# First transfers, warm-up products and one fill, rearranged at the head of a three-block transformer kernel

## The reference

```
Qh = split(layernorm(x) @ Wq.T + bq)      # 16 heads of 8
Kh = split(ctx @ Wk.T + bk);  Vh = split(ctx @ Wv.T + bv)
scores = einsum('bhqd,bhkd->bhqk', Qh, Kh) / sqrt(8)
attn = softmax(scores - max(scores));  attn = clip(attn, 1e-12)
attn = attn / sum(attn)
x = x + merge(einsum('bhqk,bhkd->bhqd', attn, Vh)) @ Wo.T + bo
```

## Time and profile before

| | |
|---|---|
| median of 3 runs | 210.49 us (210.32 to 210.79) |
| the profiled execution's own time | 210.37 us |
| its span, first to last instruction | 208.4 us |
| PE / DVE / ACT / POOL busy | 92% / 70% / 69% / 39% of the span |
| chain that ended last, by engine | PE 73%, DVE 13%, ACT 4%, DMA 3% |

### The profile page before, as it was taken

One profiled execution on the slowest core, in us unless ns is written; L12 is line 12 of the kernel. 1 busy time (PEld: TensorE's weight loads), 2 busy tenths in 40 slices (PEclk: granted clock), 3 DMA queues, 4 the chain that ended last, 5 costly groups with the idle time before them and its releaser, 6 DMA issues.

```text
span 208.4 us, 6357 instructions
## 1 busy us (share of the span) xinstructions
PE 190.9 (92%) x2558; PEld 132.3 (63%) x2559; DVE 145.7 (70%) x263; ACT 143.6 (69%) x321; POOL 81.5 (39%) x113
## 2 busy tenths in 40 slices
PE   4889899799999989999999999999879999999991
PEld 1335437255555545554554666897858998999981
DVE  5296488999999988999999944756984438222220
ACT  4768684488989897786796977686674545446660
POOL 6223679989899991110201001420000005078400
PEclk9999999999999999999999999999999999999999
DMA  5835332336437422327887750500000000000000
GB/s 119 285 151 216 118 98 89 93 94 228 159 101 198 122 81 82 97 67 234 277 296 211 213 190 6 203 2 0 3 0 3 0 0 13 3 0 5 0 0 20
DMA packets 8688, 21.24 MB, mean 102 GB/s; under 512 B 1664, under 2 KB 2784, under 8 KB 8656
## 3 DMA queue, kind: packets, MB, share of 16 engines
q1 hardware_dynamic: 7344, 19.47, 29.1%
q0 software_dynamic: 592, 0.74, 1.6%
q10 hardware_dynamic: 720, 0.59, 0.9%
HBM read 17.52 MB, written 3.28 MB: 100 GB/s over the span
## 4 chain that ended last, share of the span: by engine, by line
PE 73%; DVE 13%; ACT 4%; DMA 3%; issue 2%; POOL 2%; ACTq 1%; DVEq 0%
PE ps L1267 15%; PE ps L1516 13%; PE ps L1549 10%; PE ps L1248 10%; PE ps L1208 6%; PE ps L1113 4%; DVE mx L600 4%; DMA wks<-in_wk 3%; PE ps L1120 2%; PE ps L1407 2%; PE ps L1132 2%; POOL wr L496 1%; DVE sm L711 1%; PE ps L1413 1%; DVE kst L709 1%
## 5 line engine op out<-in xcount | busy, mean ns | idle before, releaser
L1025 ACT ACTIVATE ex<-ps 128x512 f32<-128x512 f32 x128 | 69.5, 595 | 15.7 <-PE ps L1248 12.8
L600 DVE TENSOR_REDUCE mx<-ps 128x2 f32<-128x1024 f32 x64 | 74.9, 1218 | 7.7 <-PE ps L1208 7.7
L1267 PE MATMUL ps<-ex,vau 128*9 128x128 f32 x1024 | 40.0, 274 | 0.5 <-ACT oS L1037 0.4
L1516 PE MATMUL ps<-xT,w1s 128*128 128x128 f32 x256 | 34.4, 278 | 0.2
L1516 PEld LDWEIGHTS ps<-xT,w1s 128*128 128x128 f32 x256 | 31.1, 192 | 1.6 <-ACT cT L1048 0.8
L1267 PEld LDWEIGHTS ps<-ex,vau 128*9 128x9 f32 x1024 | 22.1, 90 | 15.7 <-ACT ex L1025 11.8
L806 DVE SCALAR_TENSOR_TENSOR xs<-ps,wr,xs 128x128 f32<-128x128 f32 x32 | 11.2, 350 | 28.6 <-PE ps L1549 28.3
L1048 ACT ACTIVATE cT<-ps,b1s 128x128 f32<-128x128 f32 x64 | 18.2, 370 | 13.8 <-PE ps L1516 13.8
L1048 ACT ACTIVATE ex<-ps,b1s 128x128 f32<-128x128 f32 x64 | 18.1, 369 | 13.0 <-PE ps L1516 12.9
L1208 PE MATMUL ps<-kst,qst 64*128 64x512 bf16 x128 | 25.0, 381 | 1.9 <-DVE mx L600 1.8
L1248 PE MATMUL ps<-qst,kst 64*128 64x128 bf16 x512 | 25.5, 217 | 0.5 <-ACT ex L1025 0.4
(11 more groups left out here) (211 smaller groups left out, 255.3 us busy)
## 6 DMA issues: line engine op xcount, KB each, us to landing
kst<-parts_d SPq DMA_DIRECT2D x84, 64.0 KB
w1s<-in_w SPq DMA_DIRECT2D x8, 512.0 KB, 4.1
kst<-in_w SPq DMA_DIRECT2D x8, 512.0 KB, 4.8
parts_d<-w1s SPq DMA_DIRECT2D x4, 768.0 KB, 3.8
cT<-in_ctxT SPq DMA_DIRECT2D x3, 512.0 KB, 5.7
cT<-in_ctxT SPq DMA_DIRECT2D x2, 256.0 KB, 4.8
picks<-in_pick ACTq DMA_DIRECT2D x1, 384.0 KB, 5.3
qkvs<-in_qkvw POOLq DMA_DIRECT2D x1, 192.0 KB, 3.6
```

Of the source, the lines that this page charges most:

```text
L600: dve.tensor_reduce(out=mx2[:, b, 2 * pair:2 * pair + 2, f], in_=ps[:, bank:bank + 2, :], axis=AX.X, op=ALU.max).then_inc(s["redA"], 1)
L1025: act.activation(ex[:, e % NE, :], ps[:, EBANK["exp", e], :], ACT.Exp, scale=SCALE).then_inc(s["exp"], 1)
L1267: last = pe.matmul(ps[32 * j:32 * j + DK + 1, 7, 128 * hg:128 * hg + 128], vau[:, NK * b + c, GH * hg + j, :], ex[:, (2 * t + j % 2) % NE, ...
L1516: last = pe.matmul(ps[:, SELF[j % 2], 128 * n:128 * n + 128], w1s[:, f0:f0 + 128], xT[:, (b % B) * S:(b % B + 1) * S], start=True, stop=True)
```

## The change

- SP issues context piece 0 ahead of `x`; ACT issues `wks` ahead of `cols` and `ident`.
- VectorE's fill of pairs 2 and 3 (2048 words) becomes three memsets: 256 words of pair 3, its other 768, the 1024 of pair 2. The first raises the semaphore that TensorE waits for, the last the one that SP waits for.
- TensorE runs eight warm-up products instead of five, on those 256 words, and `keys(0)` ahead of `turn_first`.
- ScalarE's two fills of 2048 words go; GpSimd fills pairs 4 to 7 with one memset of 4096 words, between L446 and its wait for the queries' parts.

```diff
-        N_WARM = 5
+        N_WARM = 8
@@ sync
+            sp.dma_start(cT[:, 0, 0:512], ctxT[0, :, 0:512]).then_inc(d_c[0], 16)
             sp.dma_start(xs[:], x.rearrange("b s d -> s b d")).then_inc(d_x, 16)
-            sp.dma_start(cT[:, 0, 0:512], ctxT[0, :, 0:512]).then_inc(d_c[0], 16)
             sp.dma_start(cT[:, 0, 512:1024], ctxT[0, :, 512:1024]).then_inc(d_c[1], 16)
...
-                    sp.wait_ge(s["onesD"], 1)
+                    sp.wait_ge(s["onesD"], 2)
@@ gpsimd
-            pool.memset(expo[:, 4:5].bitcast(i32), MINUS_ONES2)
...
             pool.tensor_scalar(blbk[:], blocks[:], cols[:, 1:2], None, ALU.mult)
+            pool.memset(kst[:, 0, 4:8, :].bitcast(i32), MINUS_ONES2).then_inc(s["onesA"], 1)
             pool.wait_ge(s["qparts"], 1)
@@ vector
-            dve.memset(kst[:, 0, ON_CHIP:4, :].bitcast(i32), MINUS_ONES2).then_inc(s["onesD"], 1)
+            dve.memset(kst[:, 0, 3, 0:512].bitcast(i32), MINUS_ONES2).then_inc(s["onesD"], 1)
+            dve.memset(kst[:, 0, 3, 512:CTX].bitcast(i32), MINUS_ONES2)
+            dve.memset(kst[:, 0, 2, :].bitcast(i32), MINUS_ONES2).then_inc(s["onesD"], 1)
             dve.wait_ge(d_x, 16)
             layer_norm(0)
@@ scalar
+            act.dma_start(wks[:], wk).then_inc(d_wk, 16)
             act.dma_start(cols[:], bias).then_inc(d_cols, 16)
             act.dma_start(ident[:], ident_in).then_inc(d_id, 16)
-            act.dma_start(wks[:], wk).then_inc(d_wk, 16)
...
-            act.wait_ge(s["pool"], 2)
-            for p in (4, 6):
-                last = act.activation(kst[:, 0, p:p + 2, :].bitcast(fp32).rearrange("p r k -> p (r k)"),
-                                      expo[:, 4:5].broadcast_to([128, CTX]), ACT.Copy)
-            last.then_inc(s["onesA"], 1)
@@ tensor
-                pe.matmul(ps[:, 3, :], kst[:, 0, ON_CHIP, 0:128], kst[:, 0, ON_CHIP, 0:512], start=True, stop=True)
-            turn_first()
+                pe.matmul(ps[:, 3, :], kst[:, 0, 3, 0:128], kst[:, 0, 3, 0:512], start=True, stop=True)
             pe.wait_ge(d_wk, 16)
             keys(0)
+            turn_first()
             keys(1)
```

## The result

The changed kernel takes 214.88 us (median of 4 runs, 214.48 to 223.71) against 210.64 for the kernel before: 1.0193 times as long, 95% interval 1.0169 to 1.0217. The profiled execution took 215.06 us, its span 213.1 against 208.4. The three others have a median of 214.70: the change costs 4.1 us, twice the 2.0 that were forecast.

A forecast was written before the change was run, and what follows sets the result against it. The prediction took the head's chain through the layer norm and first `k_parts` to `key_rows(0)` as the bound. 210.37 us plus 2.0 lost to the held cast gave 212.4, 212.5 as a median, range 210.0 to 214.6.

The forecast's parts named there:

- What bounds the head: First 14 us: `key_rows(0)` waits for the first `k_parts`, behind a layer norm whose 3.0 us of slack the change uses up.
- Transfers: Head of the queues: `x`, now behind context piece 0, lands at about 5.7 us; piece 0 and `wks` around 5.
- X: Time at which VectorE can start the layer norm's statistics: 3.09 us before, forecast 5.7.
- The norm: VectorE's layer norm: its own chain stays 3.79 us, so `k_parts(0)` may start at 9.52 us, against 9.91.
- Fill: GpSimd's memset of 4096 words: 3.45 us long, from 9.25 to 12.7 us.
- The hold: VectorE's cast L566 waits for the rest of GpSimd's memset, 2.4 us, making the first `k_parts` 2.0 us late.
- the maximum of the earlier trace: A VectorE maximum out of PSUM, read as 1.23 us wholly inside a GpSimd fill: that form isn't held.
- The clock: TensorE's pace in the head: the main case, chance 0.42, had a fast clock, with 211.8 to 213.6 us.
- The sum: Whole kernel: 210.37 us profiled plus 2.0 gives 212.4, or 212.5 as a median.
- the rival: TensorE slow when `key_rows(0)` starts, costing 1.8 us on top of the cast's wait: 213.6 to 215.4, chance 0.25.

The follow-up runs named there:

- a1_filler: Changed kernel with 14 more unused products on TensorE between `queries` and `key_rows(0)`: 211.95 us, ratio 1.0062 to the kernel before.
- a2: Changed kernel with GpSimd's fill moved: 3072 words ahead of its power for the first layer norm, 1024 behind `qsq`: 210.24 us, ratio 0.9973.
- a3: Changed kernel with the two fills of 2048 words back on ScalarE and GpSimd's memset out: 210.15 us, ratio 0.9962.
- b3: a2 with five unused products between `keys(0)` and `turn_first` and four between `queries` and `key_rows(0)`: 211.26 us, ratio 1.0040.
- c1: Kernel before, `x` still first, with `wks` at the head of ScalarE's queue and ten early warm-up products: 213.44 us, ratio 1.0050.
- b1: Changed kernel with GpSimd's fill of 4096 words cut into 16 memsets of 256 words in the same place: 215.36 us, ratio 1.0221.
- b4: Kernel before with only the early warm-up: VectorE's fill in three memsets, nine products from 1.18 us on: 211.07 us, ratio 1.0030.
- c3: a2 without any warm-up product (`N_WARM = 0`): 212.65 us.
- d1: Kernel before with one line moved, `cols` behind `wks` in ScalarE's queue: 209.80 us, ratio 0.9953.
- a4_before_fill: Kernel before with only the fill moved from ScalarE to GpSimd, in the place the change gives it: 210.71 us, ratio 1.0022.
- b2: Changed kernel with half of GpSimd's fill (2048 words) in its place and the other half behind `qsq`: 212.56 us, ratio 1.0110.
- c2: Kernel before with one edit, `wks` at the head of ScalarE's queue: 210.88 us, ratio 1.0033.

## Why the prediction was wrong, by its steps

*What bounds the head.* Right: the layer norm, which had 3 us of slack, became the bound, and `k_parts(0)` behind it. *Transfers.* X was given as 5.7 (5.0 to 6.8) and is 5.44; `keys(0)` at 5.04 (5.1). *The norm.* `k_parts(0)` starts at X + 3.46 and not X + 3.82: the transposes ran at the fast level (0.44 us in place of 0.69), and the subtraction began 0.08 us ahead of the end of the copy. *Fill.* 3.45 forecast, 3.51 measured; start at X + 3.31 for X + 3.55. *The hold.* 2.4 forecast, 2.43 measured, and it ends with the fill as the rows of L540 had said. The rule of the Trainium skill ("SBUF — State Buffer", "Who interferes with whom"), that a VectorE cast in a two-port mode and a GpSimd instruction shut each other out for a whole instruction, agrees with the long memset here: 2.86 in place of 0.43. One reading on the way was off: the maximum of the earlier trace rows lay not wholly inside the fill, which ended at 24.35, 0.34 us ahead of it. Beside 0.9 us of the fill it took its usual 1.23, so the conclusion stands. Together these steps give `key_rows(0)` 1.41 us late, forecast 2.0; a1_filler, in which only they are left, came out at 211.95, and the forecast was 212.5.

*The clock* is the step that failed, twice. The sum has no term for it: the clock was to stay up through the pause ahead of `key_rows(0)`. It stood only as a rival, "if it is slow when `key_rows(0)` starts", given 0.25 against 0.42 for a clock that stays. The three executions of the ratio took 214.5 to 215.1, as the rival would have them (213.6 to 215.4), and the trace shows the clock falling 0.4 us behind a pause that the forecast had itself worked out ("up to 3.4 us"; 3.60 measured). The pause looked like a place where nothing is lost, since the chain waits for VectorE there. And the rival's price was put at 1.8 us, half of a slow stretch as long as the one before had. The stretch was 6.8 us long, not 3.6, and it cost 3.2: 1.4 us of the error come from that. The forecast borrowed the length from a place where TensorE had been at work, with two short pauses, for 4 us already; that this is why it was shorter there is not shown. With the terms as measured the sum is 212.5 - 0.6 (`x` and the norm came sooner than forecast) + 3.2 (the clock) = 215.1, and the traced execution took 215.06. The median of 214.88 lies 0.3 above the range given, which ended at 214.6, inside the rival's own.

That the gain in the better runs is small (a2, a3) is the layer norm again: of 1.98 us by which `keys(0)` came sooner, 1.0 reached VectorE.

*Still open:* why the clock rises by 7 us in some traces and between 10 and 20 in others of nearly the same order, and what happened in b3's and c1's high runs. The kernel before has high runs too: none of 19 beside b1 to b4, but two of nine at 215.0 and 215.4 beside c1 to c3, and four of 17 at 211.8 to 212.5 beside d1. The page "TensorE: Matmul & The Clock Gate", Part 1, of the Trainium skill says that the rise falls at different points from run to run. The spread of b4 and a4_before_fill would fit that, 209.84 to 212.44 and 210.36 to 213.78 for one program each, but no program was traced twice, so no run here shows the rise itself move.

## What to carry to other kernels

A transfer moved to the front pushes another back: work out how long the displaced one's own chain is (here 3.8 us of layer norm) and what stands behind it on each engine. An engine that waits "for free" is not free if it is TensorE in front of a dense stretch: such a pause turned a loss of 1.4 us into 4.1. And before work goes to GpSimd because it idles, look at which doubled-rate VectorE operations it will run beside; splitting it into pieces that follow each other without a wait doesn't help (b1), while doing half of it later does shorten the hold (b2).

## What was not expected of the hardware

- Sixteen memsets of 256 words, issued back to back, held VectorE's cast for 3.0 us, until the last had ended; the cast never got in between.
- The fall of the clock is not tied to the pause in one way. In the changed kernel it came when TensorE had gone back to work: `key_rows(0)` began at 13.41, and the stretch from 13 to 14 us has a mean granted clock of 0.91, the next ones 0.50.

```profile
13.00:14.00 1.00, 0.59 (x6) 0.25 (x6) 0.95 (x3) 0.00 (x0) 0.00 (x0) 0.91 0.04 16
15.00:16.00 1.00, 1.00 (x2) 0.00 (x0) 0.93 (x3) 0.66 (x1) 0.92 (x2) 0.50 0.00 0
```

  In b1, whose TensorE is idle from 9.97 to 14.17, it fell within the pause, at about 12.5:

```profile
12.00:13.00 1.00, 0.00 (x0) 0.00 (x0) 1.00 (x1) 0.00 (x0) 1.00 (x5) 0.76 0.61 246
13.00:14.00 1.00, 0.00 (x0) 0.00 (x0) 0.97 (x3) 0.00 (x0) 0.02 (x1) 0.50 0.18 74
```

- Nor does the length of the last pause decide it. In the traces of a3 and b2 the clock fell 0.2 and 1.1 us behind pauses of 1.92 and 1.90 us; in d1's it stayed up through one of 2.13 us.
- 64 KB at the third place of a queue landed 1.5 us later than at the second: `wks` took 5.3 us to land from its issue in the kernel before and 4.3 in d1, where it was issued 0.5 us sooner, so it gained 1.5 in all for 2 KB moved behind it (one trace of each). `ident`, third in c1 and c2, took 5.3 us too.
